# Recurrence stage: token transposes moved between gate tiles, Gelu behind the second tile, scaled input on VectorE

## The chip, the cores and the metric

The kernel runs on one core of one Trainium2 chip. The metric is the device time of one execution in microseconds (us), given as the median of three runs. The kernel before takes 1444.91 us (1443.92 to 1445.85). The profile comes from one further execution of 1442.83 us.

## The reference, cut to what matters

Six layers run one after the other on 8 batches of 256 tokens of 256 numbers: window attention, cross attention and a mixture of experts, then a gated linear recurrence, a second cross attention and a binarized feed-forward. Each ends in a residual and a layer norm. Only the recurrence is touched:

```python
gi = jnp.einsum('btd,hd->bth', x, W_in)
gate, xc = jnp.split(gi, 2, axis=-1)          # 512 channels each
...                                           # xc: causal convolution over time, 4 taps, plus conv_b
g = jnp.einsum('bth,gh->btg', xc, W_g) + b_g
forget, inp = jnp.split(g, 2, axis=-1)
alpha = jnp.exp(ALPHA_LOG_SCALE * jax.nn.softplus(forget_base) * jax.nn.sigmoid(forget))
beta = jnp.sqrt(1.0 - alpha ** 2 + 1e-06)
bterm = beta * jax.nn.sigmoid(inp) * xc
_, h = lax.associative_scan(_scan_combine, (alpha, bterm), axis=1)
out = jnp.einsum('bth,dh->btd', jax.nn.gelu(gate, approximate=False) * h, W_out)
```

and the layer is `x = layernorm(x + out)`.

## The kernel before, in words

The recurrence works batch by batch, 512 channels as four tiles of 128 partitions, time (256) along the free dimension. Every engine has its own program, written out by hand as a function `batch(b, ...)`; `both` unrolls batch 0 and the last three and loops over the others in pairs. Semaphores order the engines. An engine executes its list strictly in the order written. Pairs of tiles share one 128x512 buffer, called p = 0 and p = 1.

In `batch(b)` the engines work on three neighbouring batches at once:

- TensorE: `way_in(b+1)` first transposes the tokens of batch b+1 (4 transposes of 128x128, L2251) into one PSUM bank, waits until ScalarE has copied them to SBUF (`x_ready`), and multiplies them with W_in (32 matmuls, L2260). Then come gate tiles 0 and 1 of batch b (16 matmuls each, L2272), `way_out(b-1)` (16 matmuls, L2280), and gate tiles 2 and 3 of batch b.
- ScalarE: `tokens(b+1)` is the copy of the transposed tokens (L2089). `conv_input(b+1)` copies the half that is convolved (L2096). `root(b-1)` is a square root for beta (L2124). `gates(b+1)` is Gelu (L2103) and waits until the outputs of batch b-1 are gated. Then `tile(b, m)` for the four tiles: two Tanh from PSUM (L2110 forget, L2113 input), a Tanh (L2117) and an Exp (L2118). Sqrt, Gelu and Exp need different tables, which a table load brings in. Tanh is run without a load behind Gelu as well as behind Exp.
- VectorE: `convolve(b+1)` of pair 0 (8 instructions, L2173 and L2176), `enter(b+2)` (adds the experts' output to the tokens and takes statistics, L2155), `scan` and gating of batch b-1 (L2192, L2196), `convolve` of pair 1, `enter_norm(b+2)` (writes the normed tokens, L159), `residual(b-1)` (L2201), and `decay(b)` (L2183, L2185, L2186), with `layer_norm(b-1)` between its pairs.
- GpSimd: fetches the experts' rows of batch b+3 (indirect DMA, L2035), `times_beta(b-1)` (L2056), the inverse square roots of both norms (L155), and `scale_input(b)` for both pairs: ti*conv (L2048), then + conv (L2050), which is twice sigmoid(inp)*xc.
- SyncE: `stage(b)` (L2009) waits for `enter_norm(b)` and copies the tokens from the table X into the buffer `xs[b % 2]`, from which TensorE transposes.

The scan of batch b-1 waits for bterm from GpSimd, `way_out(b-1)` waits for the gated scan, and gate tile 0 of batch b waits for the convolution of batch b, which was finished during batch b-1.

Of the kernel before, what the change touches and what calls it, by code (L numbers as in the profile page):

```python
# [23 lines left out]
ALU = mybir.AluOpType  # L24
# [1899 lines left out]
def recurrence(nc, gates, slots, slot, ident, half, X, next_loads):  # L1924


    with ExitStack() as ctx:
# [51 lines left out]
        T_done = sem("T_done")  # L1979
        chain = sem("chain")  # L1980
        beta_ready = sem("beta_ready")
        doubled = sem("doubled")
        scaled_ready = sem("scaled_ready")
        bterm_ready = sem("bterm_ready")
        scanned = sem("scanned")
# [32 lines left out]
        @block.gpsimd  # L2018
        def _(pool):
            pool.memset(tiny[:], 0.25e-6).then_inc(consts, 1)  # L2020

            def fetch(b, par):

                def passes(n):

                    pool.tensor_tensor(carry[:, 2 * par + n:2 * par + n + 1], half[:], half[:], ALU.add)

                if not (isinstance(b, int) and b < 2):
                    pool.wait_ge(entered, (b - 1) * TPB)
                    passes(0)  # L2030
                pool.tensor_copy(where[par][:], slot[:, bass.ds(b * TPB, TPB)]).then_inc(pointed, 1)
                pool.wait_ge(pointed, b + 1)
                passes(1)
                for t in range(TPB):
                    pool.indirect_dma_start(out=y[par][:, t], out_offset=None, in_=slots.rows[:, :],  # L2035
                                            in_offset=bass.IndirectOffsetOnAxis(ap=where[par][:, t:t + 1], axis=0)).then_inc(gathered[par], 16)

            def root_in(b):
                norm_in.root(pool, b, 0)
                norm_in.root(pool, b, 1)  # L2040

            def scale_input(b, par, p):

                c = conv[par][:, 2 * p:2 * p + 2]
                pool.wait_ge(ti_done, b * HT + 2 * p + 2)
                if not first(b):
                    pool.wait_ge(bterm_ready, 2 * b + p - 1)
                pool.tensor_tensor(scaled[p][:], ti[p][:], c, ALU.mult).then_inc(doubled, 1)  # L2048
                pool.wait_ge(doubled, 2 * b + p + 1)
                pool.tensor_tensor(scaled[p][:], scaled[p][:], c, ALU.add).then_inc(scaled_ready, 1)  # L2050

            def times_beta(b, p):

                pool.wait_ge(scaled_ready, 2 * b + p + 1)
                pool.wait_ge(beta_ready, 2 * b + p + 1)
                pool.tensor_tensor(bterm[p][:], scaled[p][:], beta[p][:], ALU.mult).then_inc(bterm_ready, 1)  # L2056

            def batch(b, par, before=True, after=True, enters=True, fetches=True):
                if fetches:
                    fetch(b + 3, 1 - par)  # L2060
                if before:
                    times_beta(b - 1, 0)
                    times_beta(b - 1, 1)
                if enters:
                    root_in(b + 2)
                if before:
                    norm.root(pool, b - 1, 0)
                    norm.root(pool, b - 1, 1)
                scale_input(b, par, 0)
                scale_input(b, par, 1)  # L2070

            for b in (0, 1):
                fetch(b, b)
            root_in(0)
            root_in(1)
            fetch(2, 0)
            both(batch)(pool)
            times_beta(BATCH - 1, 0)
            times_beta(BATCH - 1, 1)
            norm.root(pool, BATCH - 1, 0)  # L2080
            norm.root(pool, BATCH - 1, 1)

        @block.scalar
        def _(act):
            act.wait_ge(consts, 1)

            def tokens(b):
                act.wait_ge(x_turned, b + 1)
                act.activation(xt[:], x_bank[:], ACT.Copy).then_inc(x_ready, 1)  # L2089

            def conv_input(b):
                if not first(b):
                    act.wait_ge(conved, b * TAPS * HT)
                for p in range(2):
                    act.wait_ge(in_done, 4 * b + p + 1)
                    act.activation(padded[:, 2 * p:2 * p + 2, TAPS - 1:], i_bank[p][:], ACT.Copy).then_inc(in_read, 1)  # L2096

            def gates(b, par):
                if not (isinstance(b, int) and b < 2):
                    act.wait_ge(gated, 2 * b - 2)  # L2100
                for p in range(2):
                    act.wait_ge(in_done, 4 * b + 2 + p + 1)
                    act.activation(gate[par][:, 2 * p:2 * p + 2], i_bank[p][:], ACT.Gelu).then_inc(in_read, 1)  # L2103

            def tile(b, m):
                p, k = divmod(m, 2)
                act.wait_ge(g_done, b * HT + m + 1)
                if not (first(b) and m < 2):
                    act.wait_ge(T_done, b * HT + m - 1)
                act.activation(tf[:, k], g_bank[m][:, 0], ACT.Tanh, scale=0.5, bias=half_bias[:, 0, m:m + 1]).then_inc(tf_done, 1)  # L2110
                if not first(b):
                    act.wait_ge(scaled_ready, 2 * b + p - 1)
                act.activation(ti[p][:, k], g_bank[m][:, 1], ACT.Tanh, scale=0.5, bias=half_bias[:, 1, m:m + 1]).then_inc(ti_done, 1)  # L2113
                act.wait_ge(tf_done, b * HT + m + 1)
                if not first(b):
                    act.wait_ge(chain, 6 * b + 3 * p - 5)
                act.activation(T[p][:, k], tf[:, k], ACT.Tanh, scale=rate[:, m:m + 1], bias=rate[:, m:m + 1])  # L2117
                act.activation(E[p][:, k], tf[:, k], ACT.Exp, scale=minus_twice[:, m:m + 1],  # L2118
                               bias=minus_twice[:, m:m + 1]).then_inc(T_done, 1)

            def root(b, p):

                act.wait_ge(chain, 6 * b + 3 * p + 2)
                act.activation(beta[p][:], nb[p][:], ACT.Sqrt, scale=-0.25, bias=tiny[:]).then_inc(beta_ready, 1)  # L2124

            def batch(b, par, before=True, after=True, enters=True, fetches=True):
                if after:
                    tokens(b + 1)
                    conv_input(b + 1)
                if before:  # L2130
                    root(b - 1, 0)
                    root(b - 1, 1)
                if after:
                    gates(b + 1, 1 - par)
                for m in range(HT):
                    tile(b, m)

            tokens(0)
            conv_input(0)
            gates(0, 0)  # L2140
            both(batch)(act)
            root(BATCH - 1, 0)
            root(BATCH - 1, 1)

        @block.vector
        def _(dve):
# [16 lines left out]
            def convolve(b, par, p):  # L2163

                dve.wait_ge(in_read, 4 * b + p + 1)
                if not (isinstance(b, int) and b < 2):
                    dve.wait_ge(scaled_ready, 2 * b - 2)
                for tap in range(TAPS):
                    for k in range(2):
                        m = 2 * p + k  # L2170
                        out, x, w = conv[par][:, m], padded[:, m, tap:tap + SEQ], hid[:, tap, m:m + 1]
                        if tap == 0:
                            ins = dve.tensor_scalar(out, x, w, hid[:, TAPS, m:m + 1], ALU.mult, ALU.add)  # L2173
                        else:
                            dve.wait_ge(conved, b * TAPS * HT + TAPS * 2 * p + 2 * tap + k - 1)
                            ins = dve.scalar_tensor_tensor(out=out, in0=x, scalar=w, in1=out, op0=ALU.mult, op1=ALU.add)  # L2176
                        ins.then_inc(conved, 1)

            def decay(b, p):

# [28 lines left out]
            def batch(b, par, before=True, after=True, enters=True, fetches=True):  # L2209
# [10 lines left out]
                    enter_norm(b + 2)  # L2220
                if before:
                    residual(b - 1)
                decay(b, 0)
                if before:
                    layer_norm(b - 1)
                decay(b, 1)

            for b in (0, 1):
# [12 lines left out]
        def _(pe):  # L2241
            pe.wait_ge(gates.w_loaded, 48)

            def way_in(b, par):

                pe.wait_ge(staged[par], 8 * (b - par) + 16)
                if not first(b):
# [1 line left out]
                for g in range(KT_):  # L2249
                    for t in range(TPB):  # L2250
                        ins = pe.transpose(x_bank[:, g, t * P:(t + 1) * P], xs[par][:, t, g * P:(g + 1) * P], ident[:])  # L2251
                ins.then_inc(x_turned, 1)
                pe.wait_ge(x_ready, b + 1)
                for s in range(4):
                    if not (first(b) and s < 2):
# [26 lines left out]

            def batch(b, par, before=True, after=True, enters=True, fetches=True):
                if after:
                    way_in(b + 1, 1 - par)
                tile(b, par, 0)
                tile(b, par, 1)
                if before:
                    way_out(b - 1)
                tile(b, par, 2)  # L2290
                tile(b, par, 3)

            way_in(0, 0)
            both(batch)(pe)
            way_out(BATCH - 1)

# [410 lines left out]
```

## Time and profile before

| what | value |
|---|---|
| median of 3 runs | 1444.91 us |
| the profiled execution | 1442.83 us, of which the span is 1441.1 us |
| outside the span | 1.73 us |
| TensorE busy over the span | 1212.0 us (84%) |
| VectorE busy | 1043.9 us (72%) |
| ScalarE busy | 731.6 us (51%) |
| GpSimd busy | 424.8 us (29%) |
| mean granted TensorE clock | 0.914 |
| first transposes of the recurrence start | 945.97 us |
| last norm of the recurrence starts | 1186.39 us |

Busy time is time in which an instruction of the engine is recorded as running. Idle time of an engine matters only where another engine cannot make up for it. The engines: PE is TensorE's matmul side, DVE is VectorE, ACT is ScalarE, POOL is GpSimd, SPq is SyncE's DMA issue. A row such as "1009.26 7.17 PE L2260 ... x32 [2.03 <-ACT re_xt L2089]" is a run of 32 instructions of line 2260 that starts at 1009.26 us and lasts 7.17 us; TensorE had been idle for 2.03 us before it, and the last thing to release it was ScalarE's copy of line 2089. TensorE's instructions are pipelined, so the next run can start a little before the recorded end of the last.

### The profile page before, as it was taken

What the parts mean: (1) busy time and instruction counts of PE and PEld (TensorE: products, weight loads), DVE (VectorE), ACT (ScalarE), POOL (GpSimd) and SP (SyncE); (2) the same over time, 40 slices, a digit from 0 to 9 for tenths busy, and PEclk for the clock granted to TensorE, in tenths of its full rate; (3) what the DMA queues carried; (4) which work ended last, traced back from release to release, by engine and by line L of the source; (5) the groups of instructions that cost most, each with busy time, mean ns of one, the idle gap of its engine ahead of it and who ended that gap; (6) DMA issues with size and microseconds to landing.
All of it is one profiled execution on the core that took longest, in us unless ns stands there. A gap on an engine that the chain in (4) does not pass through costs nothing. (4 is left out here: it accounts for less than half of the span.)

```text
span 1441.1 us, 28676 instructions
## 1 busy us (share of the span) xinstructions
PE 1212.0 (84%) x9867; PEld 967.8 (67%) x9867; DVE 1043.9 (72%) x2297; ACT 731.6 (51%) x1446; POOL 424.8 (29%) x478
## 2 busy tenths in 40 slices
PE   3789897998989887999654999779998958999697
PEld 1467776777677775777543777557887746777485
DVE  6588777786777854888674787357888754888587
ACT  3454444454444523655372777425556614565384
POOL 4212021211202003555304000035544333555323
PEclk7799999999999997999855999879999977999799
DMA  5000000010000004000153443130000000000011
GB/s 200 8 2 9 3 7 10 1 63 1 3 2 1 2 1 167 21 19 17 42 243 135 145 162 104 46 105 16 23 15 15 1 0 22 21 19 17 30 45 44
DMA packets 33924, 64.35 MB, mean 45 GB/s; under 512 B 7574, under 2 KB 23446, under 8 KB 30742
## 3 DMA queue, kind: packets, MB, share of 16 engines
q1 hardware_dynamic: 32278, 58.70, 11.6%
q0 software_dynamic: 1536, 4.20, 0.9%
q8 instruction: 67, 1.10, 0.3%
q14 instruction: 43, 0.35, 0.1%
HBM read 42.12 MB, written 12.39 MB: 38 GB/s over the span
## 5 line engine op out<-in xcount | busy, mean ns | idle before, releaser
L345 POOL TENSOR_TENSOR wa_rot<-wa_raw,wa_cos_sin 128x1024 f32<-128x1024 f32 x32 | 80.5, 2517 | 344.4 <-ACT wa_raw L389 342.0
L891 POOL TENSOR_TENSOR ca_z<-ca_z,ca_top 128x308 f32<-128x308 f32 x128 | 92.5, 722 | 136.6 <-DVE ca_top L1020 136.3
L639 PE MATMUL wa_scores<-wa_kt,wa_qt 128*128 128x192 f32 x512 | 119.3, 346 | 0.0
L2272 PE MATMUL re_g<-re_conv,re_w_g 128*128 128x256 f32 x512 | 112.8, 379 | 0.0
L963 ACT ACTIVATE ca_pth<-ca_turned 77x512 f16<-77x512 f32 x128 | 75.8, 592 | 61.3 <-PE ca_turned L1147 60.7
L2272 PEld LDWEIGHTS re_g<-re_conv,re_w_g 128*128 128x128 f32 x512 | 97.3, 190 | 13.2
L1147 PE MATMUL ca_turned<-ident,ca_probs 128*77 128x128 f32 x512 | 85.1, 290 | 20.5 <-ACT ca_probs L955 19.4
L1138 PE MATMUL ca_scores<-ca_km,ca_q 128*128 128x308 f32 x256 | 91.0, 439 | 5.9 <-ACT ca_q L936 5.7
L605 PE MATMUL wa_shared<-wa_wh,wa_xh 128*128 128x512 f16 x192 | 75.1, 391 | 19.5 <-ACT wa_raw L389 10.2
L1025 DVE SCALAR_TENSOR_TENSOR ca_ptl<-ca_turned,ca_pth 77x512 f16<-77x512 f32 x128 | 86.6, 676 | 2.6 <-ACT ca_pth L963 2.6
L639 PEld LDWEIGHTS wa_scores<-wa_kt,wa_qt 128*128 128x128 f32 x512 | 79.0, 195 | 12.9 <-issue 0.7
L389 ACT ACTIVATE wa_raw<-wa_shared 128x512 f32<-128x512 f32 x64 | 38.1, 597 | 93.7 <-PE wa_shared L605 93.7
L526 DVE SCALAR_TENSOR_TENSOR wa_ptl<-wa_turned,wa_pth 128x384 f16<-128x384 f32 x128 | 65.6, 551 | 23.0 <-ACT wa_pth L430 21.8
L955 ACT ACTIVATE ca_probs<-ca_z 128x308 f32<-128x308 f32 x128 | 58.2, 455 | 44.5 <-POOL ca_z L891 43.4
L468 DVE TENSOR_TENSOR wa_sine<-wa_raw,wa_cos_sin 128x512 f32<-128x512 f32 x64 | 63.6, 1035 | 21.4 <-ACT wa_raw L389 11.7
L613 PE MATMUL wa_shared<-ident,wa_rot 128*128 128x128 f32 x256 | 42.4, 298 | 42.1 <-DVE wa_vl L480 37.3
L503 DVE TENSOR_REDUCE wa_top<-wa_scores 128x2 f32<-128x384 f32 x128 | 70.2, 549 | 8.1 <-PE wa_scores L639 7.9
L605 PE MATMUL wa_shared<-wa_wl,wa_xh 128*128 128x512 f16 x192 | 74.8, 390 | 0.0
L605 PE MATMUL wa_shared<-wa_wh,wa_xl 128*128 128x512 f16 x192 | 74.7, 389 | 0.0
L505 DVE TENSOR_TENSOR wa_shifted<-wa_scores,wa_top 128x384 f32<-128x384 f32 x128 | 71.4, 557 | 4.4
L1147 PEld LDWEIGHTS ca_turned<-ident,ca_probs 128*77 128x77 f32 x512 | 56.7, 150 | 26.3 <-ACT ca_probs L955 22.5
L2260 PE MATMUL re_in<-re_xt,re_w_in 128*128 128x256 f32 x256 | 61.8, 403 | 13.5 <-ACT re_xt L2089 13.5
(314 smaller groups left out, 3693.1 us busy)
## 6 DMA issues: line engine op xcount, KB each, us to landing
ex_stage<-in_ew SPq DMA_DIRECT2D x16, 1024.0 KB, 6.8
slots<-slots_zeros SPq DMA_DIRECT2D x10, 512.0 KB, 5.9
ca_xs<-tokens SPq DMA_DIRECT2D x16, 256.0 KB, 2.4
ex_xe<-slots SPq DMA_DIRECT2D x11, 320.0 KB, 3.3
wa_w_stage<-in_wqkv SPq DMA_DIRECT2D x6, 512.0 KB, 4.4
slots<-ex_y SPq DMA_DIRECT2D x9, 320.0 KB
wa_x_stage<-in_xt SPq DMA_DIRECT2D x8, 256.0 KB, 3.4
tokens<-in_x SPq DMA_DIRECT2D x1, 2048.0 KB, 10.5
```

Source lines behind the costliest of these rows:

```text
L345: pool.tensor_tensor(rot[:, r % 2], raw[:, r % 2], c, ALU.mult).then_inc(cos_done, 1)
L503: dve.tensor_reduce(top[:, k], s_bank[t][:, :, 0:SPAN], AX.X, ALU.max).then_inc(maxed, 1)
L505: dve.tensor_tensor(shifted[k][:], s_bank[t][:, :, 0:SPAN], top[:, k].unsqueeze(2).broadcast_to((P, 2, SPAN)), ALU.subtract).then_inc(shif ...
L526: dve.scalar_tensor_tensor(out=windows(ptl[k][:]), in0=windows(t_bank[h][:]), scalar=PSCALE, in1=windows(pth[k][:]), op0=ALU.mult, op1=ALU ...
L605: ins = pe.matmul(dst[:], a[:, par, k, tok], w[:, k, cols], start=(k == 0 and n == 0), stop=(k == KT_ - 1 and n == 2))
L639: ins = pe.matmul(dst, qt[par][:, 2 * u + h, t * P:(t + 1) * P], kt[par][:, u, t * WINDOW:t * WINDOW + SPAN], start=False, stop=True)
L891: pool.tensor_tensor(z[k][:], z[k][:], top[:, k].unsqueeze(2).broadcast_to((P, UH, CTX)), ALU.subtract).then_inc(shift, 1)
L963: act.activation(pth[k][0:CTX], t_bank[k][0:CTX], ACT.Copy, scale=PSCALE).then_inc(probs_high, 1)
L1025: dve.scalar_tensor_tensor(out=ptl[k][0:CTX], in0=t_bank[k][0:CTX], scalar=PSCALE, in1=pth[k][0:CTX], op0=ALU.mult, op1=ALU.subtract).then ...
L1138: pe.matmul(s_bank[c % 2][:, 0:UH * CTX], q[par][:, g, t * P:(t + 1) * P], km[par][:, g, h:h + UH].rearrange("p h k -> p (h k)"), start=Tr ...
L1147: ins = pe.transpose(t_bank[k][0:CTX, h * P:(h + 1) * P], probs[k][:, h], ident[:])
L2272: ins = pe.matmul(g_bank[m][:, k], w_g[:, j, cols], conv[par][:, j], start=(j == 0), stop=(j == HT - 1))
```

## The change

On TensorE the transposes leave `way_in` and become `turn`, called for batch b+2 between gate tiles 2 and 3 of batch b. On ScalarE the copy of the transposed tokens follows tile 2, also for batch b+2, and `gates(b+1)` moves from in front of tile 0 to behind tile 1. GpSimd's two instructions per pair of `scale_input` become one on VectorE, (ti + 1)*conv, in front of each `decay`. The semaphore between the two GpSimd instructions goes.

```diff
@@ gpsimd @@
-            def scale_input(b, par, p):
-
-                c = conv[par][:, 2 * p:2 * p + 2]
-                pool.wait_ge(ti_done, b * HT + 2 * p + 2)
-                if not first(b):
-                    pool.wait_ge(bterm_ready, 2 * b + p - 1)
-                pool.tensor_tensor(scaled[p][:], ti[p][:], c, ALU.mult).then_inc(doubled, 1)
-                pool.wait_ge(doubled, 2 * b + p + 1)
-                pool.tensor_tensor(scaled[p][:], scaled[p][:], c, ALU.add).then_inc(scaled_ready, 1)
...
-                scale_input(b, par, 0)
-                scale_input(b, par, 1)
@@ scalar, batch @@
                 if after:
-                    tokens(b + 1)
                     conv_input(b + 1)
                 if before:
                     root(b - 1, 0)
                     root(b - 1, 1)
+                tile(b, 0)
+                tile(b, 1)
                 if after:
                     gates(b + 1, 1 - par)
-                for m in range(HT):
-                    tile(b, m)
+                tile(b, 2)
+                if enters:
+                    tokens(b + 2)
+                tile(b, 3)
 
             tokens(0)
             conv_input(0)
             gates(0, 0)
+            tokens(1)
@@ vector @@
+            def scale_input(b, par, p):
+
+                dve.wait_ge(ti_done, b * HT + 2 * p + 2)
+                if not first(b):
+                    dve.wait_ge(bterm_ready, 2 * b + p - 1)
+                dve.scalar_tensor_tensor(out=scaled[p][:], in0=ti[p][:], scalar=1.0, in1=conv[par][:, 2 * p:2 * p + 2],
+                                         op0=ALU.add, op1=ALU.mult).then_inc(scaled_ready, 1)
...
+                scale_input(b, par, 0)
                 decay(b, 0)
                 if before:
                     layer_norm(b - 1)
+                scale_input(b, par, 1)
                 decay(b, 1)
@@ tensor @@
-            def way_in(b, par):
+            def turn(b, par):
...
                 ins.then_inc(x_turned, 1)
+
+            def way_in(b):
+
                 pe.wait_ge(x_ready, b + 1)
...
                 if after:
-                    way_in(b + 1, 1 - par)
+                    way_in(b + 1)
                 tile(b, par, 0)
                 tile(b, par, 1)
                 if before:
                     way_out(b - 1)
                 tile(b, par, 2)
+                if enters:
+                    turn(b + 2, par)
                 tile(b, par, 3)
 
-            way_in(0, 0)
+            turn(0, 0)
+            way_in(0)
+            turn(1, 1)
```

## Rows read from the trace of the kernel before

**Rows 1.** Windows: stretch, us, busy (count) PE, PEld, DVE, ACT, POOL; clock, DMA, GB/s.
```profile
1009.00:1036.00 27.00, 24.87 (x116) 21.71 (x116) 23.21 (x53) 15.19 (x27) 14.41 (x16) 1.00 0.07 21
1117.00:1145.00 28.00, 28.00 (x123) 24.36 (x123) 19.93 (x41) 14.88 (x26) 9.17 (x8) 0.94 0.00 1
```

**Rows 2.** Timeline of TensorE: start us, us, engine, line, what, [idle before <-releaser].
```profile
979.73 0.60 PE L2251 MATMUL re_x<-ident,re_xs 128*128 128x128 f32 x4
982.36 7.17 PE L2260 MATMUL re_in<-re_xt,re_w_in 128*128 128x256 f32 x32 [2.03 <-ACT re_xt L2089]
...
1009.26 7.17 PE L2260 MATMUL re_in<-re_xt,re_w_in 128*128 128x256 f32 x32 [2.03 <-ACT re_xt L2089]
...
1023.18 3.62 PE L2280 MATMUL re_out<-re_w_out,re_gh 128*128 128x256 f32 x16
1026.63 7.07 PE L2272 MATMUL re_g<-re_conv,re_w_g 128*128 128x256 f32 x32
1033.54 0.60 PE L2251 MATMUL re_x<-ident,re_xs 128*128 128x128 f32 x4
```

**Rows 3.** Timeline of ScalarE: tile 1 of batch 0, and batch 2.
```profile
974.25 0.59 ACT L2118 ACTIVATE re_E<-re_tf,re_minus_twice 128x256 f32<-128x256 f32 x1
...
1024.89 0.48 ACT L2110 ACTIVATE re_tf<-re_g,re_half_bias 128x256 f32<-128x256 f32 x1
...
1026.22 1.28 ACT L2118 ACT_TABLE_LOAD   x1
...
1028.02 0.45 ACT L2110 ACTIVATE re_tf<-re_g,re_half_bias 128x256 f32<-128x256 f32 x1
...
1033.74 0.47 ACT L2110 ACTIVATE re_tf<-re_g,re_half_bias 128x256 f32<-128x256 f32 x1 [1.64 <-PE re_g L2272]
...
1035.45 0.59 ACT L2089 ACTIVATE re_xt<-re_x 128x512 f32<-128x512 f32 x1
```

**Rows 4.** Timeline of VectorE in the same batch.
```profile
1012.01 0.74 DVE L2173 TENSOR_SCALAR re_conv<-re_padded,re_hid 128x256 f32<-128x256 f32 x2 [0.43 <-ACT re_padded L2096]
...
1015.04 0.42 DVE L2155 TENSOR_TENSOR rn_res<-re_y,tokens 128x256 f32<-128x256 f32 x1
...
1016.37 0.98 DVE L2155 TENSOR_TENSOR rn_res<-re_y,tokens 128x256 f32<-128x256 f32 x1
...
1018.26 1.34 DVE L2192 TENSOR_TENSOR_SCAN re_h<-re_alpha,re_bterm 128x256 f32<-128x256 f32 x2
...
1021.55 0.69 DVE L2196 TENSOR_TENSOR re_gh<-re_gate,re_h 128x512 f32<-128x512 f32 x1
...
1035.58 0.89 DVE L2183 SCALAR_TENSOR_TENSOR re_d<-re_E,re_T 128x512 f32<-128x512 f32 x1 [1.30 <-ACT re_E L2118]
```

**Rows 5.** VectorE's lines of decay, all batches: duration ns min/median/max, first and last start.
```profile
L2183 DVE SCALAR_TENSOR_TENSOR re_d<-re_E,re_T x16: 680/882/886, 974.9 to 1167.9; 128x512 f32<-128x512 f32 x16
...
L2185 DVE SCALAR_TENSOR_TENSOR re_nb<-re_d x16: 691/1641/1649, 975.8 to 1168.8; 128x512 f32<-128x512 f32 x16
...
L2186 DVE TENSOR_SCALAR re_alpha<-re_d x16: 412/1484/1496, 977.4 to 1170.3; 128x512 f32<-128x512 f32 x16
```

**Rows 6.** Timeline of GpSimd: scale_input of pair 1, and times_beta.
```profile
1009.10 1.59 POOL L2050 TENSOR_TENSOR re_scaled<-re_scaled,re_conv 128x512 f32<-128x512 f32 x1
...
1015.79 2.68 POOL L2056 TENSOR_TENSOR re_bterm<-re_scaled,re_beta 128x512 f32<-128x512 f32 x2 [1.43 <-ACT re_beta L2124]
```

**Rows 7.** Staging of a batch: VectorE's norm, SyncE's issue (timeline), time to landing.
```profile
1025.18 0.73 DVE L159 TENSOR_SCALAR tokens<-rn_res,rn_mv,rn_rstd 128x256 f32 x2
...
1026.04 0.49 SPq L2009 DMA_DIRECT2D re_xs<-tokens  x1
...
DMA to landing us min/median/max: 2.3/2.3/2.4
```

**Rows 8.** Timeline of the last batches: ScalarE's load behind the root, TensorE's last-but-one way_out.
```profile
1148.07 1.28 ACT L2110 ACT_TABLE_LOAD   x1
...
1153.66 5.41 PE L2280 MATMUL re_out<-re_w_out,re_gh 128*128 128x256 f32 x16 [3.90 <-DVE re_gh L2196]
```

More of the change, by code:

```diff
@@ L1981, in recurrence @@
         beta_ready = sem("beta_ready")
-        doubled = sem("doubled")
         scaled_ready = sem("scaled_ready")
```

## The prediction

> **What bounds the kernel now.** I read the stage's windows first, then TensorE's timeline, then the other engines' timelines around each of its gaps. In the 27 us window of a steady batch TensorE is busy 24.87 us at full granted clock, VectorE 23.21, ScalarE 15.19, GpSimd 14.41 [rows 1]. So TensorE sets the pace, but VectorE has little room. TensorE's timeline shows where its 2 us go: `way_in` starts at 982.36 and again at 1009.26, a period of 26.90, with one hole of 2.03 before it, between the transposes and W_in's matmuls [rows 2]. The hole is a round trip. The last gate tile ends where the transposes begin (1033.54), ScalarE is still in the Tanh and Exp of tile 3 (from 1033.74) and reaches the copy only at 1035.45 [rows 3]; W_in follows 0.72 behind the copy's start, at 1033.54 + 0.60 + 2.03 = 1036.17. There are six such holes (batches 2 to 7; batch 1's is in the prologue), 12.2 us in all.
>
> I write W for the start of `way_in`, S for that of `way_out`, M for the moment when gate tile 3 is through and the next TensorE work could start. Before, S = W + 13.92 and M = S + 10.36 (3.45 for `way_out`, 6.91 for two gate tiles) [rows 2].
>
> **Transposes and copy two batches ahead.** The 4 transposes still cost TensorE 0.60, now between tiles 2 and 3, so M = S + 10.96. The copy hangs on ScalarE's tile 2: its first Tanh starts 0.20 behind its matmuls, S + 3.45 + 3.46 + 0.20 = S + 7.11. A tile with the Exp table load takes 3.13 (1024.89 to 1028.02), and copy to matmul is 0.72 [rows 3], so `way_in` may start at S + 10.96: equal to M. The hole goes, and both engines arrive together. Without any other limit the period would be 26.90 - 2.03 = 24.87.
>
> The new order adds a wait in TensorE's queue: `turn` waits for the staged tokens and tile 3 stands behind it. Before, the norm of these tokens ran at 1025.18, the DMA was issued at 1026.04 and landed 2.3 later, about 1028.4 [rows 7], which is 5.2 behind S. The transposes now want them at S + 6.91. The slack is some 1.7, and as the norm follows the gating that also releases `way_out`, it shrinks only to about 0.9 when `way_out` waits. I cost it at nothing.
>
> **Gelu behind tile 1.** Before, Gelu's table served the Tanh of tile 0, and a load came at the Exp. Now the order Sqrt, tiles 0 and 1, Gelu, tiles 2 and 3 needs four loads a batch for three, at 1.28 each [rows 3]. At the end of the stage, where tiles follow the root without Gelu, one load at L2110 serves them [rows 8]; so tiles 0 and 1 take one, early, while ScalarE waits for matmuls. Gelu's load and two passes (about 2.5) lie under `way_out` (3.45). Only the load at tile 2's Exp is on the path, and it is in the 3.13. In batch 0 there is no `way_out`: Exp of tile 1 ends at 974.84, then 1.28 + 2 x 0.59, so tile 2 starts some 0.7 late, and W with it. The next batch has that much slack between W and S, and gets it back. ScalarE goes from 15.2 to 16.5 of 25: hidden.
>
> A rule speaks against this. The trace shows a load of 1.28, and the Exp ready right behind it [rows 3]. The Trainium skill (ScalarE: Activation LUTs, "What ACT_TABLE_LOAD costs") adds a drain of about 1.38 us to each switch. With it the copy would come 1.4 later and the period would be that of before; by the row it costs nothing more, and I go by the row.
>
> **Scaled input on VectorE.** GpSimd loses two instructions per pair, of which one took 1.59 [rows 6]. VectorE gains one per pair; the nearest form is L2183, same shape, two SBUF inputs: 0.68 free, 0.88 disturbed [rows 5], so 1.4 a batch. It runs at M + 1.1, when the input Tanh of tile 3 is out, while the Exp comes at M + 2.0: it fits in the idle 1.30 before L2183 [rows 4]. The bounds are 0 and 2 x 1.64.
>
> What it gives back is larger. L2185 takes 0.69 at best and 1.64 in the middle, L2186 0.41 and 1.48 [rows 5]. The L2185 of batch 1 stands next to GpSimd's L2050, 1009.10 to 1010.69 [rows 6]. The long ones lie beside GpSimd's work on tensors: the one engine waits the other out. With `scale_input` off GpSimd the decay runs free: about 0.95 less for L2185 in each, and 1.07 for L2186 in pair 0.
>
> **The new limit: VectorE from tile 3 to `way_out`.** With the hole gone, decay of pair 1, convolution, entry and scans no longer have its 2.03 us. From M: Exp ends +2.01, L2183 starts +2.04 [rows 4]; L2183, L2185 and L2186 free take 0.71 + 0.61 + 0.33 start to start, so the convolution starts at +3.69. It takes 3.03 (1012.01 to 1015.04) [rows 4]: +6.72. There the entry's first add meets `times_beta`, which GpSimd asks for at W + 6.53 (1015.79 - 1009.26), 1.34 each [rows 6]. Before, one add was held: 0.98 against 0.42 [rows 4]. Now I count both. GpSimd gets in when the convolution's last instruction is done, +6.81, and holds 1.26 (the 1.34 less what it waited itself): the add ends 0.22 behind it at +8.29, the second is asked for 0.91 later, at +9.20, and held by the second product until about +9.77. The scans follow 0.91 behind (1016.37 + 0.98 to 1018.26), +10.68, and scans and gating take 3.98 (1018.26 to 1021.55 + 0.69) [rows 4]: +14.66. TensorE takes 0.06 from the gating to `way_out` (seen at 1153.66), so S = M + 14.72, where W + 13.92 was free. TensorE waits 0.8 there, and the period is 14.72 + 10.96 = 25.68.
>
> The Trainium skill (SBUF — State Buffer, "Who interferes with whom") says that VectorE with two SBUF inputs and a GpSimd instruction that reads SBUF exclude each other for the whole instruction. The rows above agree (1.64 for 0.69); without such a lock the add would take 0.42 and S would be free.
>
> **The sum.** First hole 2.03; five periods (batches 1 to 5) from 26.90 to 25.68, 1.22 each, 6.1. In batch 6 nothing is entered, and S stays with TensorE. In the tail two chains Exp, decay, scan, `way_out` stand open (TensorE waits 3.90 before 1153.66 [rows 8]); the decay is 0.95 shorter, but the products of GpSimd still come at the root's pace, so 0.5 each, 1.0 (bounds 0 and 2). Together 9.1. From the profiled 1442.83: 1433.7. The median lies 2.1 above that execution, so 1435.8.
>
> **The rivals.**
> - A, TensorE alone is the limit: the adds slip past GpSimd. Period 24.87, 12.2 - 0.7 + 1.0 = 12.5 off: 1432.4. For it: VectorE is over by 0.8 only, and that is made of two holds. Against: the second add is held in every steady batch.
> - B, the convolution loses the lock: if its last instruction is asked for later than W + 6.53, GpSimd takes 1.3 in front of it and again in front of the adds. My last start is M + 6.33, a margin of 0.2. S = M + 15.5, period 26.45, 2.0 + 5 x 0.45 + 1.0 = 5.3 off: 1439.6.
> - C, the copy is late, because tile 2's chain takes a second table load or the drain (1.3 to 1.4). Period 26.9 to 27.0, only the tail's 1.0 and some of the first hole left: 1442.9. Against: tile 0 had the same neighbours before, and shows one load.
> - D, slower: `turn` waits for its tokens, and tile 3 and all of ScalarE's tile 3 behind it. With a slack of 0.9, each us of landing beyond 3.2 costs one in each of six batches; it is slower than before from a landing of 4.9. At 5.5, 2.3 x 6 = 13.8 against 9.1: 1449.6. Against: the transfer landed in 2.3 to 2.4 in all eight batches, and nothing else of SyncE's moves near it.
> - E, the clock takes the gain: in 1117 to 1145 it was 0.94 in the mean, and TensorE was never idle there [rows 1]. 28 x 0.06 = 1.7 us is such a dip. Five more of them, here or in the stages behind, would leave no difference; one fewer gives 1434.1.
>
> **Chances.** Forecast 0.45, A 0.20, B 0.20, C 0.05, D 0.03, E 0.07. About 0.2% (2.9 us) is what can be told from no change: faster takes the forecast, A, B and a bit of E, 0.87; same C and most of E, 0.09; slower D and a rest for what I don't see, 0.04. The range goes from A with one dip fewer, 1430.5, to a little past B, 1441.0.
>
> **What would show it.** The hole before L2260 gone or under 0.2, and a new one before L2280 with L2196 as its releaser: 0.8 (none in A, 1.6 in B). `way_in` to `way_in` 25.7. L2185 near 0.69 and L2186 near 0.41 throughout; L2155 near 1 in both adds. Four table loads a batch, none at tile 3. The DMA of `stage` landed before `turn`, with no idle at L2251. The forecast is wrong if the period stays above 26.5 or VectorE isn't the one that `way_out` waits for.

## The result and the profile after

The changed kernel takes 1432.96 us (median of 9 executions, 1430.32 to 1437.36), the kernel before, also in 9 executions, 1444.91 us: a ratio of 0.9925, with an interval of 0.9905 to 0.9944, or 8 to 14 us less. The forecast was 1435.8. The profiled execution took 1430.32, with a span of 1428.6 against 1441.1.

The rows of TensorE's timeline that answer to [rows 2], start, length, instruction, [idle before <-releaser]:

```profile
977.37 0.60 PE L2252 MATMUL re_x<-ident,re_xs 128*128 128x128 f32 x4
977.80 3.62 PE L2276 MATMUL re_g<-re_conv,re_w_g 128*128 128x256 f32 x16
982.07 7.17 PE L2264 MATMUL re_in<-re_xt,re_w_in 128*128 128x256 f32 x32 [0.65 <-ACT re_xt L2076]
...
1003.32 3.62 PE L2276 MATMUL re_g<-re_conv,re_w_g 128*128 128x256 f32 x16
1006.93 7.17 PE L2264 MATMUL re_in<-re_xt,re_w_in 128*128 128x256 f32 x32
...
1020.84 3.62 PE L2284 MATMUL re_out<-re_w_out,re_gh 128*128 128x256 f32 x16
...
1031.80 7.17 PE L2264 MATMUL re_in<-re_xt,re_w_in 128*128 128x256 f32 x32
...
1106.23 7.17 PE L2264 MATMUL re_in<-re_xt,re_w_in 128*128 128x256 f32 x32
```

The hole in front of `way_in` is gone, the period is 1031.80 - 1006.93 = 24.87, and `way_out` stands 13.91 behind `way_in`, against 13.92 before. `way_out` waits for nothing in a steady batch, and `way_in` starts 0.07 to 0.16 later than TensorE's own work would let it. The 0.65 that is left is batch 0's.

VectorE's and GpSimd's timelines of the same batch, which answer to [rows 4, 6]:

```profile
1009.55 0.69 DVE L2184 SCALAR_TENSOR_TENSOR re_nb<-re_d 128x512 f32<-128x512 f32 x1
...
1010.50 0.73 DVE L2164 TENSOR_SCALAR re_conv<-re_padded,re_hid 128x256 f32<-128x256 f32 x2
...
1011.15 2.46 DVE L2167 SCALAR_TENSOR_TENSOR re_conv<-re_padded,re_hid,re_conv 128x256 f32<-128x256 f32 x6
...
1013.46 3.02 POOL L2045 TENSOR_TENSOR re_bterm<-re_scaled,re_beta 128x512 f32<-128x512 f32 x2 [6.54 <-ACT re_beta L2111]
1013.52 0.41 DVE L2146 TENSOR_TENSOR rn_res<-re_y,tokens 128x256 f32<-128x256 f32 x1
...
1014.84 0.51 DVE L2146 TENSOR_TENSOR rn_res<-re_y,tokens 128x256 f32<-128x256 f32 x1
...
1019.55 0.69 DVE L2195 TENSOR_TENSOR re_gh<-re_gate,re_h 128x512 f32<-128x512 f32 x1
```

nb takes 0.69 where it mostly took 1.64 [rows 5]. The two adds of the entry are hardly held. It is GpSimd that waits: its pair takes 3.02 instead of 2.68, and the first product of the pair 1.61 where it takes 1.27 alone. The gating ends at 1020.24, 0.6 before `way_out`. The scaled input and alpha on VectorE, all batches:

```profile
L2175 DVE SCALAR_TENSOR_TENSOR re_scaled<-re_ti,re_conv x16: 692/693/694, 975.0 to 1154.2; 128x512 f32<-128x512 f32 x16
...
L2185 DVE TENSOR_SCALAR re_alpha<-re_d x16: 418/420/422, 977.3 to 1156.5; 128x512 f32<-128x512 f32 x16
```

Where the time came from, between the two profiled executions:

| stretch | before | after | less |
|---|---|---|---|
| start of way_in(0) to way_in(2) | 34.55 | 33.26 | 1.3 |
| way_in(2) to way_in(7), five periods | 134.36 | 124.16 | 10.2 |
| way_in(7) to way_out(6) | 36.94 | 34.78 | 2.2 |
| way_out(6) to way_out(7) | 23.09 | 22.64 | 0.45 |
| way_out(7) to the last norm | 9.64 | 9.95 | -0.3 |

That is 13.8 us in the stage. The stage began 1.0 later and the stages behind took 0.3 longer, which leaves the 12.5 of the span. Of the 2.2, 1.7 is one slow `way_in` of before (8.86 us against 7.17), whose granted clock was 0.80 in the mean; the same stretch ran at 1.00 after. From the trace of before:

```profile
1116.72 8.86 PE L2260 MATMUL re_in<-re_xt,re_w_in 128*128 128x256 f32 x32 [1.95 <-ACT re_xt L2089]
```

### The profile page after: what moved, and what is told of

Read it like the earlier page. It is cut to its first block and busy times, and to the rows that moved or that the text cites. A ratio compares the mean times of both kernels' runs of the same rounds, so it can differ in the third digit from the quotient of the medians.

```text
span 1428.6 us, 28658 instructions
## 1 busy us (share of the span) xinstructions
PE 1213.4 (85%) x9867; PEld 967.9 (68%) x9867; DVE 1025.0 (72%) x2313; ACT 743.3 (52%) x1454; POOL 380.5 (27%) x446
## 5 line engine op out<-in xcount | busy, mean ns | idle before, releaser
L650 PE MATMUL wa_turned<-ident,wa_probs 128*128 128x128 f32 x512 | 70.8, 284 | 0.0
```

What stands on the lines that cost most here:

```text
L650: ins = pe.transpose(t_bank[h][:, j * SEQ + t * P:j * SEQ + (t + 1) * P], probs[2 * (u % 2) + t][:, h, j * P:(j + 1) * P], ident[:])
```

## The experiments

Two theories stood. By the first, the gain is TensorE's hole, and the other two edits only keep VectorE and ScalarE out of its way. By the second, each edit is worth something, or nothing, by itself. A table behind the last experiment sets the stage alone of every variant beside the others; where it tells more than the median does, the text says so.

**The transposes and the copy alone.** Undone from the changed kernel: the scaled input (two instructions on GpSimd again, the body of `scale_input` as before) and

```diff
+                if after:
+                    gates(b + 1, 1 - par)
                 tile(b, 0)
                 tile(b, 1)
-                if after:
-                    gates(b + 1, 1 - par)
                 tile(b, 2)
```

> The kernel before with the transposes and the copy moved alone; Gelu stands in front of tile 0 and the scaled input is on GpSimd, as before. Theory T (the gain is the hole, and the other two edits are what lets TensorE keep it): VectorE's chain from tile 3 to way_out is longer by about 1.2 us (decay waits for GpSimd) and by up to another 1.2 if GpSimd's product gets in front of the convolution's last instruction; TensorE waits before way_out, the period is 25.5 to 26.7, the kernel 2 to 8 us under before. Rival H (the hole alone counts, the other edits are worth nothing): period 24.9, 11 to 12 us under before.

Measured: 1447.94 us against 1446.64 for the kernel before, ratio 1.0027 (1.0010 to 1.0045): slower, if by little. The holes before `way_in` are gone, and larger ones stand before `way_out`, as TensorE's timeline shows:

```profile
1013.89 7.07 PE L2267 MATMUL re_in<-re_xt,re_w_in 128*128 128x256 f32 x32
...
1031.23 5.41 PE L2287 MATMUL re_out<-re_w_out,re_gh 128*128 128x256 f32 x16 [3.37 <-DVE re_gh L2200]
...
1043.83 7.07 PE L2267 MATMUL re_in<-re_xt,re_w_in 128*128 128x256 f32 x32
```

This period is 29.9; the five run from 27.2 to 30.1. The rival that the hole alone counts is out, and the first theory was wrong on the size and on the sign of the whole: it allowed a period of 26.7 and expected 2 to 8 us less. The total hides how much slower the stage is. In the profiled executions it takes 247.6 us against 240.4, 7.2 more, and the stages behind it, whose code is the same, 249.0 against 254.7 at a mean granted clock of 0.95 against 0.92. Why they ran faster is open.

**The scaled input back on GpSimd, all else changed.**

```diff
+                scale_input(b, par, 0)       # GpSimd, behind the roots, two instructions each
+                scale_input(b, par, 1)
@@ vector @@
-                scale_input(b, par, 0)
                 decay(b, 0)
...
-                scale_input(b, par, 1)
                 decay(b, 1)
```

> The changed kernel with the scaled input put back on GpSimd as two instructions. Theory T: L2185 of before (nb) goes back to about 1.6 us, the convolution starts 1.2 later, TensorE waits before way_out: period 25.5 to 26.7, 3 to 9 us slower than the changed kernel. Rival H: the slack of 0.5 us and GpSimd's turn-taking absorb it; period 24.9, no difference but 1 us in the tail.

Measured: 1449.37 us, ratio 1.0037 (1.0016 to 1.0059), some 14 to 16 us above the changed kernel where 3 to 9 were expected. In the traces the stage is 21 us longer than the changed kernel's, and again the stages behind took some 6 less. Its VectorE and GpSimd in a steady batch, in order of time:

```profile
1043.81 1.64 DVE L2189 SCALAR_TENSOR_TENSOR re_nb<-re_d 128x512 f32<-128x512 f32 x1
...
1045.71 0.73 DVE L2177 TENSOR_SCALAR re_conv<-re_padded,re_hid 128x256 f32<-128x256 f32 x2
...
1046.35 5.29 DVE L2180 SCALAR_TENSOR_TENSOR re_conv<-re_padded,re_hid,re_conv 128x256 f32<-128x256 f32 x6
...
1047.69 1.14 POOL L2035 DMA_INDIRECT re_y<-slots,re_where  x1 [0.30 <-ACT re_beta L2124]
...
1048.86 2.49 POOL L2056 TENSOR_TENSOR re_bterm<-re_scaled,re_beta 128x512 f32<-128x512 f32 x2
...
1058.30 5.41 PE L2287 MATMUL re_out<-re_w_out,re_gh 128*128 128x256 f32 x16 [3.22 <-DVE re_gh L2200]
```

nb is back at 1.64 and the convolution starts about 1.1 later (4.9 behind the end of gate tile 3, against 3.7), as expected. Then its last six instructions take 5.29 instead of 2.46: while GpSimd forms both of its products, the last instruction of VectorE's convolution stands. It starts at 1048.33, half a us in front of the products, while GpSimd's gather of the experts' rows (L2035) still runs, and takes 3.31 for 0.48. So it is in all four batches in which that gather comes directly in front of the products. In the last two, which fetch nothing, the six take 4.48. Some 0.8 of the hold therefore goes with the gather, which `scale_input` makes late; in the changed kernel it is through 6.5 us before the products. The variant of the first experiment shows the same two figures. TensorE waits 3.22, and then runs `way_out` in 5.41 instead of 3.62.

**Is it the lateness alone?** The changed kernel, with nothing but idle memsets in front of the first convolution, in three lengths.

```diff
+                    for k in range(2):                       # 1 for the two shorter delays
+                        dve.memset(spare[:, 480 * k:480 * k + 480], 0.0)   # 240 for the shortest
                     convolve(b + 1, 1 - par, 0)
```

> The changed kernel with two idle memsets of 128x480 on VectorE in front of each batch's first convolution, some 0.3 to 1 us in all; nothing else changed, and GpSimd has only its products. Theory L (lateness alone brings the convolution under GpSimd's products): from a delay of about 0.3 us on, the six instructions behind the first two take 3.8 to 5.3 us instead of 2.46, way_out waits for the gating, TensorE's clock falls there, and the period goes to 26 to 30. Rival D (the slow convolution of the variant with scaled input on GpSimd came of GpSimd's other work): the convolution keeps its 2.46, way_out is late by the delay less 0.5 us, period 24.9 to 25.4.

> The same with one memset of 128x480, about 0.48 us. Theory L: the last convolution instruction is queued behind GpSimd's product and held 1.2 to 2.0; way_out waits 1 to 2 us, period 26 to 27. Rival D: 0.48 is inside the slack, period 24.9.

> The changed kernel with one idle memset of 128x240 on VectorE in front of each batch's first convolution, about 0.25 us. Two such of 128x480 were 0.96 us. Theory L: the last instruction of the convolution now starts about when GpSimd asks for its first product, so either nothing is held and way_out keeps up (slack 0.5), or one product (1.3) gets in front of the first add; period 24.9, or up to 25.8 with the hold. Rival D (the slack of 0.5 us is all that counts, lateness comes through one to one): period 24.9 and nothing held.

Measured, one execution each, beside the kernel before at 1445.96 (long) and 1445.36 (the others): long 1445.91, half 1428.98, short 1426.22. With one execution each, the argument goes by the traces and not by these times. The long one, VectorE and GpSimd:

```profile
1043.40 0.96 DVE L2212 MEMSET re_spare<- 128x480 f32 x2
1044.29 0.55 DVE L2165 TENSOR_SCALAR re_conv<-re_padded,re_hid 128x256 f32<-128x256 f32 x2
1044.75 4.49 DVE L2168 SCALAR_TENSOR_TENSOR re_conv<-re_padded,re_hid,re_conv 128x256 f32<-128x256 f32 x6
1046.26 2.70 POOL L2046 TENSOR_TENSOR re_bterm<-re_scaled,re_beta 128x512 f32<-128x512 f32 x2 [6.68 <-ACT re_beta L2112]
```

A delay of 1.0 makes the convolution itself 2.03 longer, and the gain of the change is gone: the stage takes 240.5 us, as in the kernel before. The half delay is the sharpest of the three. Two of its batches:

```profile
1037.15 2.46 DVE L2168 SCALAR_TENSOR_TENSOR re_conv<-re_padded,re_hid,re_conv 128x256 f32<-128x256 f32 x6
1039.16 3.32 POOL L2046 TENSOR_TENSOR re_bterm<-re_scaled,re_beta 128x512 f32<-128x512 f32 x2 [6.68 <-ACT re_beta L2112]
...
1086.88 3.47 DVE L2168 SCALAR_TENSOR_TENSOR re_conv<-re_padded,re_hid,re_conv 128x256 f32<-128x256 f32 x6
1088.80 2.68 POOL L2046 TENSOR_TENSOR re_bterm<-re_scaled,re_beta 128x512 f32<-128x512 f32 x2 [10.04 <-ACT re_beta L2112]
...
1090.28 1.48 DVE L2147 TENSOR_TENSOR rn_res<-re_y,tokens 128x256 f32<-128x256 f32 x1
...
1097.73 3.72 PE L2287 MATMUL re_out<-re_w_out,re_gh 128*128 128x256 f32 x16 [1.39 <-DVE re_gh L2196]
```

In the first, the last convolution instruction (0.48 long) starts at 1037.15 + 2.46 - 0.48 = 1039.13, just 0.03 before GpSimd's product; nothing is held, and the four periods up to batch 4 are 24.8 to 24.9. In batch 5 GpSimd asks at +1.92 from the start of the six instead of +2.01: they take 3.47, the first add 1.48, `way_out` waits 1.39 and the period is 26.45. I had expected the half delay to fall over in every batch; it stood on the edge. The short one lost nothing, with periods of 24.8 to 24.9 and a stage of 226.5 us against 226.6. So lateness alone brings 2.03 of the 2.83 seen with the scaled input on GpSimd, and rival D is right about the other 0.8.

The distance in time does not settle who goes first. In the changed kernel GpSimd's first product starts at 1013.46 and the add 0.06 behind it, and the add passes. In batch 5 of the half delay the last convolution instruction is due 0.06 behind GpSimd's product as well, at 1088.86, and is held (1.49 for 0.48). What differs in the traces is where GpSimd asks. Where it asks during the last instruction of the convolution, with the add next, the add passes in every batch of the changed kernel and of the short and the half delay, up to 0.38 behind GpSimd's recorded start. Where another instruction of the convolution is next, GpSimd goes first. Why is open.

**The same long delay, with GpSimd's products on VectorE.**

```diff
-                pool.tensor_tensor(bterm[p][:], scaled[p][:], beta[p][:], ALU.mult).then_inc(bterm_ready, 1)
@@ vector, scan @@
+                dve.tensor_tensor(bterm[p][:], scaled[p][:], beta[p][:], ALU.mult).then_inc(bterm_ready, 1)
```

> The long delay (0.96 us), with GpSimd's two products of scaled input and beta moved to VectorE, one in front of each scan; GpSimd then reads no large tensor in this stage. Theory X (what holds the convolution is GpSimd's product over the shared way into SBUF): its six instructions take 2.46 again, in spite of the delay; the products cost VectorE 0.7 each instead, so way_out still waits some 1.8 us and the period is 26.4 to 27. Rival: another late operand holds the convolution; it stays near 4.5.

Measured: 1438.70 against 1445.36, one execution each, periods of 26.3 to 26.8, and a wait of 1.3 to 1.7 before `way_out`.

```profile
1040.23 0.96 DVE L2208 MEMSET re_spare<- 128x480 f32 x2
1041.12 0.55 DVE L2154 TENSOR_SCALAR re_conv<-re_padded,re_hid 128x256 f32<-128x256 f32 x2
1041.58 2.46 DVE L2157 SCALAR_TENSOR_TENSOR re_conv<-re_padded,re_hid,re_conv 128x256 f32<-128x256 f32 x6
...
1046.61 0.69 DVE L2181 TENSOR_TENSOR re_bterm<-re_scaled,re_beta 128x512 f32<-128x512 f32 x1
```

The same lateness, and the convolution takes 2.46. So it is GpSimd's products that hold it in the long delay, and no late operand. The Trainium skill (SBUF — State Buffer, "Who interferes with whom") has the rule that VectorE with two SBUF inputs contends with a GpSimd instruction that reads SBUF, and the trace agrees: the convolution's `scalar_tensor_tensor` reads two tensors in SBUF, and so does GpSimd's product.

**The scaled input alone, on the kernel before.** The `scale_input` hunks of the change, nothing else.

> The kernel before with the scaled input on VectorE alone. Theory T: the hole stays at 2.0 and the period at 26.9, because what VectorE gets back is not on the path while ScalarE's copy is; only the tail gains 0.5 twice, 1 us in all, no measurable change. Rival S (most of the gain is VectorE relieved of the shared waiting): period under 26, 5 us or more faster than before.

Measured: 1440.39 us, ratio 0.9963 (0.9946 to 0.9980), 3 to 8 us less where 1 was expected. The hole stays at 2.03 and the period at 26.90:

```profile
1013.00 7.17 PE L2257 MATMUL re_in<-re_xt,re_w_in 128*128 128x256 f32 x32 [2.03 <-ACT re_xt L2076]
...
1039.90 7.17 PE L2257 MATMUL re_in<-re_xt,re_w_in 128*128 128x256 f32 x32 [2.03 <-ACT re_xt L2076]
```

The rival, that relief of VectorE is most of the gain, is out. In the traces the stage is 2.6 shorter up to `way_out(7)`: 0.9 by the shorter waits in the tail, as said, and 1.7 as `way_out(6)` ran at a granted clock of 1.00 (3.72 for 5.41). `way_out(7)` is another 0.4 shorter, and the stages behind took 2.5 less (252.2 against 254.7), at a clock of 0.93 against 0.92; why is open. So of some 5 us, the edit's own part that the traces show is 0.9.

```profile
1156.94 3.72 PE L2277 MATMUL re_out<-re_w_out,re_gh 128*128 128x256 f32 x16 [3.45 <-DVE re_gh L2191]
```

**Gelu in front of tile 0 again, all else changed** (the diff of the first experiment, without `scale_input`).

> The changed kernel with Gelu put back in front of tile 0. Theory T: worth nothing in a steady batch. Gelu ends some 16 us behind tile 3, tiles 0 and 1 catch up before tile 2's matmuls end, and the Exp's table load is off tile 2, so the copy comes 1.3 earlier and way_in starts without the 0.15 it now waits: period 24.75 to 24.9, and the kernel within 1 us of the changed one or faster by up to 1. Rival G (Gelu ahead holds up ScalarE's tiles, and with them the copy): period over 25.2, 2 us or more slower than the changed kernel.

Measured: 1427.18 us, ratio 0.9879 (0.9856 to 0.9902) to the kernel before. The period is 24.61, and the hole of batch 0 is gone as well:

```profile
1034.79 0.58 ACT L2076 ACTIVATE re_xt<-re_x 128x512 f32<-128x512 f32 x1
...
1036.77 7.07 PE L2264 MATMUL re_in<-re_xt,re_w_in 128*128 128x256 f32 x32
...
1061.38 7.07 PE L2264 MATMUL re_in<-re_xt,re_w_in 128*128 128x256 f32 x32
```

The copy is done 1.4 before W_in's matmuls start. From way_in(1) to way_in(7) it takes 144.3 against 146.2 of the changed kernel: 0.8 less around batch 0, and 1.1 in the five periods. So the move of Gelu costs about 2 us there: it puts the Exp's table load into tile 2, in front of the copy. Rival G is out, and the theory was too careful: it said a period of 24.75 or more and at most 1 us. The median is 6 us under the changed kernel's, though the two weren't measured side by side. The traces show 2.9 in the stage, of which 0.8 is two `way_out` of the tail that ran a little faster, and 4.4 less in the stages behind, at a clock of 0.94 against 0.91. That these 4.4 come of the edit isn't shown.

**The tail.** The changed kernel's TensorE stands 3.43 before `way_out(6)`, with gate tiles 2 and 3 of batch 7 behind it in the queue:

```profile
1141.01 5.41 PE L2284 MATMUL re_out<-re_w_out,re_gh 128*128 128x256 f32 x16 [3.43 <-DVE re_gh L2195]
```

Moved, for the last batch only, on three engines:

```diff
@@ tensor, batch @@
-                if before:
+                if before and after:
                     way_out(b - 1)
...
                 tile(b, par, 3)
+                if not after:
+                    way_out(b - 1)
@@ vector: residual(6) behind decay(7, 1), layer_norm(6) behind the scans of batch 7 @@
@@ gpsimd: the roots of batch 6 behind times_beta of batch 7 @@
```

> The changed kernel, but in the last batch way_out(6) stands behind all four gate tiles, with its residual and norm behind the decay. In the changed kernel TensorE waits 3.4 us there for the gating of batch 6 and then runs way_out in 5.2 us at a lowered clock, with tiles 2 and 3 behind it. Theory: tiles 2 and 3 follow tiles 0 and 1 at once, way_out(6) is off the chain, and the stage ends 8 to 9 us earlier: 8 us under the changed kernel. Rival: VectorE's chain of batch 7 is late because the residual of batch 6 now stands in front of its scans, and only 3 to 5 us come.

> The same, with Gelu put back in front of tile 0. Theory: both gains add, as one is in the steady batches and the first hole (2 us in the stage) and the other in the tail (8 to 9): 10 us under the changed kernel.

> The changed kernel once more, on the same chip as the others of this group, to set them against. It should stand about 0.75% under the kernel before, as it did.

Measured, 4 executions each, with the kernel before at 1445.96: the changed kernel 1434.61 (ratio 0.9911, 0.9880 to 0.9943), the tail 1419.51 (0.9819, 0.9789 to 0.9848), the tail with Gelu ahead 1417.60 (0.9804, 0.9775 to 0.9833). TensorE in the tail version:

```profile
1123.01 20.88 PE L2282 MATMUL re_g<-re_conv,re_w_g 128*128 128x256 f32 x96
1143.73 3.62 PE L2290 MATMUL re_out<-re_w_out,re_gh 128*128 128x256 f32 x16
1154.22 5.97 PE L2290 MATMUL re_out<-re_w_out,re_gh 128*128 128x256 f32 x16 [6.88 <-DVE re_gh L2197]
```

From the start of way_in(7) to that of the last `way_out` it takes 1154.22 - 1105.64 = 48.6 against 1163.65 - 1106.23 = 57.4 in the changed kernel: 8.8 less, as expected. The medians say 15. In the profiled executions the last `way_out` ran 0.7 faster and the stages behind the recurrence took 252.1 against 255.0, at a mean clock of 0.93 against 0.91, together 3.6 of the other 6; why, is open. Both versions are faster than both kernels. That Gelu ahead adds its 2 us on top is inside the interval of the medians (1.9), but the traces show it: periods of 24.6, and a stage of 214.4 against 217.2, of which 0.7 is a faster last `way_out`.

**The stage alone.** From the first transposes to the last norm of the recurrence, and from there to the end, in the profiled execution of each kernel:

| kernel | periods | stage | behind it | clock behind it |
|---|---|---|---|---|
| before | 26.8 to 26.9 | 240.4 | 254.7 | 0.92 |
| changed | 24.8 to 24.9 | 226.6 | 255.0 | 0.91 |
| changed, once more | 24.8 to 24.9 | 226.6 | 254.9 | 0.92 |
| transposes and copy alone | 27.2 to 30.1 | 247.6 | 249.0 | 0.95 |
| scaled input back on GpSimd | 27.2 to 30.0 | 247.8 | 248.9 | 0.95 |
| short delay | 24.8 to 24.9 | 226.5 | 249.5 | 0.94 |
| half delay | 24.8 to 26.5 | 227.3 | 252.2 | 0.94 |
| long delay | 26.9 to 28.7 | 240.5 | 255.0 | 0.92 |
| long delay, no products on GpSimd | 26.3 to 26.8 | 233.3 | 255.2 | 0.91 |
| scaled input alone | 26.8 to 28.5 | 237.4 | 252.2 | 0.93 |
| Gelu in front again | 24.6 | 223.8 | 250.6 | 0.94 |
| tail | 24.8 to 24.9 | 217.2 | 252.1 | 0.93 |
| tail, Gelu in front | 24.6 | 214.4 | 251.4 | 0.94 |

The code behind the stage is the same in all of them, and yet it took between 248.9 and 255.2 us, in the main the less the higher its clock. That is half the size of the gain. A median of the whole kernel therefore says less about an edit in this stage than the trace of the stage does.

## Why the prediction was right, and where not

- *The hole of 2.03 goes*: right. Five periods gave 2.04 each, where the forecast had 1.22 and rival A 2.03; the first gave 1.3, because tile 2 of batch 0 is late behind Gelu, by 0.65 where 0.7 was said. It is not given back: that would have taken an S that waits for VectorE, and S now simply follows `way_in` by 13.9.
- *Copy and matmuls arrive together at S + 10.96*: right, 1031.80 - 1020.84 = 10.96. But the 0.60 of the transposes is 0.43 on TensorE's queue (977.37 to 977.80), so its own end was S + 10.8, and the copy is the limit by 0.07 to 0.16. A `way_in` that waited also takes 0.1 longer (7.17 against 7.07 with Gelu in front). Together that is what Gelu's move costs in each batch: 0.26 in the first three periods, 0.17 in the last two.
- *The drain set against the row, and rival C*: four loads of 1.28 a batch, as said, and the Exp starts right behind its load (load at 1004.42 for 1.28, Exp at 1005.72). No further 1.4 is paid. Rival C's sum was wrong as it stood: a copy 1.3 to 1.4 late gives 24.87 + 1.3 to 1.4 = 26.2 to 26.3, and not the period of before.
- *`turn` at nothing*: right. The norm of the tokens ran at 1023.18, the DMA was issued at 1024.04 and landed some 2.3 later, 1.4 before the transposes at 1027.75.
- *Scaled input 0.7 on VectorE, nb 0.69, alpha 0.41*: right, 0.69, 0.69 and 0.42 in all 16.
- *The new limit, S = M + 14.72, with a wait of 0.8 before `way_out`*: this step failed, and by the forecast's own sign, since VectorE isn't what `way_out` waits for. With M at 1003.32 + 3.46 = 1006.78, the convolution started at +3.72 (+3.69 said) and the first add at +6.74 (+6.72). Then I had GpSimd go ahead of both adds. GpSimd had indeed asked at 1013.46, W + 6.53 as said, during the convolution's last instruction, and the add, which came 0.06 behind it, still went first. The adds took 0.41 and 0.51, and the gating ended at +13.46 instead of +14.66. So the two holds, which the forecast had at 1.3 together, were worth 0.1. This is rival A, given 0.20: period 24.87, as it says.
- *The tail, 1.0*: 0.47 and 0.45, right; 1.7 more came from the clock.
- *Rival B* was priced right at its edge and too low beyond it. In batch 5 of the half delay it happened as described: `way_out` starts at 1097.73, 15.5 behind M = 1082.20, and the period is 26.45, both as B says. A convolution that is later still is held by both products: in the long delay `way_out` starts 16.3 behind M in the batch shown, and the gain is gone. With the scaled input on GpSimd it starts 17.45 behind M, `way_out` waits 2.1 to 3.2 in five batches, three of which then run it in 5.3 to 5.4 at a granted clock of some 0.68, and the kernel is slower than before, not 5 us faster. The margin that I put at 0.2 is 1013.46 - (1011.15 + 2.46 - 0.48) = 0.33: 0.15 more, as `way_in` starts that much behind M.
- *Smaller sums*: A with one dip fewer is 1432.4 - 1.7 = 1430.7, not 1430.5. D is slower than before from a landing of 3.2 + 9.1 / 6 = 4.7, not 4.9. Neither touches the result.

The median of 1432.96 is A's 1432.4 and lies 2.8 under the forecast. That the forecast came so near is in part luck. Its period was too long by 0.81, 4.1 us in five batches. Against that stand 0.7 of the first hole that it counted and didn't get, and 1.3 that the rest of the execution took more; the clock's 1.7 (E with one dip fewer) went the other way. The nearness to A is partly luck too: in the profiled executions the clock's 1.7 less and the 1.3 more outside the stage nearly cancel.

## What to carry to other kernels

A hole on the bounding engine is often also the slack of another: take it away and look at what now meets in time. Here 1 us of lateness on VectorE cost the bounding engine 2.1 to 3.8 us a batch, and 2.4 to 5.2 where GpSimd also had the scaled input, since the late instructions ran into GpSimd's, and the edit that seems a mere move of load (two GpSimd instructions to one VectorE instruction) is what lets the reordering pay. Before moving work "out of the way" on a third engine, check that it had been in the way: Gelu was not, and its move cost a table load in front of the copy. And the end of a pipeline deserves its own order: the steady batch's put a wait of 3.4 us and a slow `way_out` in front of work that was ready.

## What the runs showed of the hardware

- A GpSimd product over two 128x512 tensors and a VectorE instruction with two inputs in SBUF wait each other out. A convolution instruction takes 0.48 alone and 1.49 behind one product of 1.27, and 3.31 where GpSimd's gather ends directly in front of both products. Without the products on GpSimd all six take 2.46 together at the same lateness. Alpha, a `tensor_scalar` with one input, was held beside GpSimd's work as well (0.41 and 1.48 [rows 5]).
- A delay of 0.5 us on VectorE cost nothing in four periods and 1.7 us in the fifth; 1.0 us cost 2.1 to 3.8 in each, with the clock.
- An add that was due 0.06 behind GpSimd's recorded start went first, a convolution instruction due 0.06 behind it was held. What decides is open. Once GpSimd was in, both of its products passed in front of the waiting convolution in the long delay (2.70 to 2.80 for the pair) and with the scaled input on GpSimd (2.49 to 2.89).
- TensorE's clock after a wait: the same 16 matmuls of `way_out` take 3.62 without one, and 3.72 (granted clock 1.00) or 5.2 to 6.5 (0.68 in the mean for 5.41, 0.56 for 6.47) after waits of 1.3 to 3.5. In the long delay a wait of 1.88 was followed by 5.41 and one of 1.98 by 3.72; with the transposes and the copy alone, one of 3.51 by 3.72. So length alone doesn't decide.
